# Two transformer layers on one core: a written order for the last groups, Sinkhorn scaling by two vectors, and a shifted sum in the mixing loop

## What is computed

```python
x = x + _L0_attn_ref(_layernorm(x), ...)   # 32 heads of 32, 8 key/value heads, causal, interleaved rope
x = x + _L0_ffn_ref(_layernorm(x), ...)    # the mixing layer
x = x + _L1_attn_ref(_layernorm(x), ...)   # the same attention, rope by halves
x = x + _L1_ffn_ref(_layernorm(x), ...)    # base matmul and 8 gated low-rank experts
```

```python
def sinkhorn_log(logits, num_iters=50, tau=0.1):
    Z = logits / tau
    def step(carry, _):
        u, v = carry
        u = -logsumexp(Z + v[..., None, :], axis=-1)
        v = -logsumexp(Z + u[..., :, None], axis=-2)
        return ((u, v), None)
    return exp(Z + u[..., :, None] + v[..., None, :])

H_res = (1.0 - g) * I + g * sinkhorn_log(H_res_logits)
y = einsum('btnc,btn->btc', x_streams, H_pre) @ W_branch
x_mixed = einsum('btij,btjc->btic', H_res, x_streams)
out = x_mixed + einsum('btc,btn->btnc', y, H_post)
```

## Time and profile before

| | |
|---|---|
| median of 3 runs | 2916.91 us |
| profiled execution, its own time | 2913.83 us |
| its span | 2912.1 us, 50930 instructions |
| PE busy | 2608.1 us (90%) |
| DVE busy | 1797.7 us (62%) |
| ACT busy | 1095.2 us (38%) |
| POOL busy | 1123.9 us (39%) |
| mean granted TensorE clock | 0.952 |
| attention 0, first score to last group's end | 116.4 to 958 us |
| mixing layer's Sinkhorn loop | 1203.9 to 1383 us |
| mixing loop | 1384 to 1464 us |
| attention 1, first score | 1582.8 us |

### The profile page before, as it was taken

One profiled execution on the slowest core, in us unless ns is written; L12 is line 12 of the kernel. 1 busy time (PEld: TensorE's weight loads), 2 busy tenths in 40 slices (PEclk: granted clock), 3 DMA queues, 4 the chain that ended last, 5 costly groups with the idle time before them and its releaser, 6 DMA issues. The chain is left out here.

```text
span 2912.1 us, 50930 instructions
## 1 busy us (share of the span) xinstructions
PE 2608.1 (90%) x15312; PEld 1828.1 (63%) x15312; DVE 1797.7 (62%) x4437; ACT 1095.2 (38%) x2381; POOL 1123.9 (39%) x801
## 2 busy tenths in 40 slices
PE   7999997999998799791969999979999987997999
PEld 6665653765654588681857565537656544876887
DVE  5677775667775433588756777765677753215543
ACT  2345454145555211470622454541354553002000
POOL 7456553546564100000054656545466642002110
PEclk9999998999999999896979999989999998998999
DMA  4323222422321421000244232213232314434111
GB/s 158 110 78 93 84 61 66 140 84 80 98 77 38 168 72 58 1 1 0 98 151 124 74 103 67 82 66 120 80 104 77 93 40 152 147 109 149 71 60 44
DMA packets 121086, 253.05 MB, mean 87 GB/s; under 512 B 12720, under 2 KB 39728, under 8 KB 120880
## 3 DMA queue, kind: packets, MB, share of 16 engines
q1 hardware_dynamic: 120912, 251.03, 27.0%
HBM read 166.57 MB, written 84.41 MB: 86 GB/s over the span
## 5 line engine op out<-in xcount | busy, mean ns | idle before, releaser
L617 ACT ACTIVATE a_prob<-a_pst 128x512 f32<-128x512 f32 (+3 forms) x1536 | 660.6, 493 | 560.4 <-PE a_pst L898 555.1
L710 DVE CUSTOM_DVE_ANT_0 a_psh<-a_psh,a_edge 128x128 f32<-128x128 f32 (+3 forms) x1024 | 479.7, 516 | 193.6 <-PE a_psh L851 172.6
L898 PE MATMUL a_pst<-a_qst,a_kst 128*128 128x512 f32 (+2 forms) x1536 | 487.9, 372 | 24.0 <-DMA a_qst<-rowmax 19.0
L851 PE MATMUL a_psh<-a_kst,a_qst 127*128 127x512 f32 (+3 forms) x1536 | 484.2, 363 | 16.2 <-DVE a_mx L710 6.1
L517 POOL TENSOR_TENSOR a_prob<-a_prob 128x2048 f32<-128x2048 f32 (+1 forms) x96 | 405.6, 4226 | 239.7 <-PE a_ppv L914 239.7
L851 PEld LDWEIGHTS a_psh<-a_kst,a_qst 127*128 127x128 f32 x1536 | 272.0, 189 | 229.8 <-DVE a_mx L713 92.7
L713 DVE TENSOR_REDUCE a_mx<-a_psh 128x1 f32<-128x512 f32 x512 | 329.1, 685 | 124.7 <-PE a_psh L851 123.7
L898 PEld LDWEIGHTS a_pst<-a_qst,a_kst 128*128 128x128 f32 x1536 | 287.5, 194 | 167.1 <-ACT a_prob L617 104.3
L914 PE MATMUL a_ppv<-a_prob,a_vg 128*32 128x512 f32 (+3 forms) x3072 | 319.8, 503 | 0.0
L502 POOL TENSOR_SCALAR_AFFINE_SELECT a_prob<-a_prob 128x512 f32<-128x512 f32 x256 | 161.8, 639 | 192.3 <-ACT a_prob L617 192.2
L927 PE MATMUL a_pden<-a_prob,a_ones 128*32 128x512 f32 (+3 forms) x2304 | 222.5, 479 | 14.1 <-POOL a_prob L517 14.1
(11 more groups left out here) (231 smaller groups left out, 4208.3 us busy)
## 6 DMA issues: line engine op xcount, KB each, us to landing
a_qst<-q SPq DMA_DIRECT2D x192, 256.0 KB, 4.5
a_wraw<-in_wqkv SPq DMA_DIRECT2D x52, 512.0 KB, 4.3
q<-a_stg_hi SPq DMA_DIRECT2D x64, 256.0 KB, 2.1
q<-a_stg_lo SPq DMA_DIRECT2D x64, 256.0 KB, 2.4
a_kst<-kT SPq DMA_DIRECT2D x96, 128.0 KB, 2.5
oT<-a_oT SPq DMA_DIRECT2D x32, 256.0 KB, 2.4
oT<-a_vT SPq DMA_DIRECT2D x32, 256.0 KB, 2.9
h_oraw<-oT SPq DMA_DIRECT2D x16, 512.0 KB, 4.0
```

The lines of the kernel that those rows point to most:

```text
L617: act.activation(prob[k % len(prob)][:, h, off:], pst[:, (k * GH + h) % 3, off:], ACT.Exp, scale=scale).then_inc(s["exp_done"], 1)
L710: part = dve.tensor_tensor_reduce(scores, scores, edge[:, BANK - n:], 1.0, 2 * MASKED, ALU.add, ALU.max, mx_hq[kc][:, h, qt:qt + 1])
L851: mm = pe.matmul(psh[:, at, i * n:(i + 1) * n], qst[par][0:P - 1, h, qt * P:(qt + 1) * P], kst[par][0:P - 1, kc * BANK:kc * BANK + n], sta ...
L898: pe.matmul(pst[:, (k * GH + h) % 3, off:], kst[par][:, ki * P:(ki + 1) * P], qst[par][:, h, qc * BANK + off:(qc + 1) * BANK], start=True, ...
```

## The change

Three edits.

1. ORDER_7, a text of its own, sets the last group of both batches; last_group() reads it, for body7 without its X and P steps. ("P:n.i" is P:next.i.) Rules and the branch of iteration() that made the old one are gone.
2. Sinkhorn keeps m unchanged in the loop and carries two vectors of 64 per partition, r64 for the rows and v64 for the columns. Each half multiplies m (or its transposed copy mt) by the other vector into e, sums e over rows and takes the reciprocal. After the loop m is multiplied by v64 and by r64, with the gate's factor in r64.
3. In the mixing loop DVE scales tile t + 1 before it adds PE's part to tile t. The first scaling and the last two sums stand outside the loop.

```diff
+ORDER_7 = """
+    ...
+    ST:3.0 XS:2 ST:3.1 ST:3.2 ST:3.3 XT:0 XL:3 D:0 XN:1 XC:0 XN:2 V:2
+    ...
+"""
...
-def iteration(full_s=True, proj=True, ahead=False):
+def iteration(proj=True):
...
+def last_group(ahead=False):
+    order = parsed(ORDER_7)
...
+    return order if ahead else [step for step in order if step[0][0] not in "XP"]
...
-    pro, bodies, body6, body7 = prologue(), (iteration(), iteration()), iteration(proj=False), iteration(False, False)
-    ahead7 = iteration(False, False, True)
+    pro, bodies, body6, body7 = prologue(), (iteration(), iteration()), iteration(proj=False), last_group()
+    ahead7 = last_group(ahead=True)
...
-            def normalise(axis):
-                dve.drain()
-                dve.tensor_reduce(r64[:, :, :], lines(m, axis), AX.X, ALU.add)
-                dve.drain()
-                dve.reciprocal(r64[:, :, :], r64[:, :, :])
-                dve.drain()
-                dve.tensor_tensor(lines(m, axis), lines(m, axis), spread(r64[:, :, :]), ALU.mult)
-            normalise("col")
+            def scale(kernel, other, out):
+                dve.drain()
+                dve.tensor_tensor(lines(e, "row"), lines(kernel, "row"), repeated(other[:, :, :]), ALU.mult)
+                dve.drain()
+                dve.tensor_reduce(out[:, :, :], lines(e, "row"), AX.X, ALU.add)
+                dve.drain()
+                dve.reciprocal(out[:, :, :], out[:, :, :])
+            dve.tensor_copy(lines(mt, "row"), lines(m, "col"))
+            dve.tensor_reduce(v64[:, :, :], lines(m, "col"), AX.X, ALU.add)
+            dve.drain()
+            dve.reciprocal(v64[:, :, :], v64[:, :, :])
             with dve.Fori(0, SINKHORN_ITERS - 1):
-                normalise("row")
-                normalise("col")
+                scale(m, v64, r64)
+                scale(mt, r64, v64)
             dve.drain()
-            dve.tensor_scalar(m[:, :, :], m[:, :, :], g[:, 2:3], None, ALU.mult)
+            dve.tensor_scalar(r64[:, :, :], r64[:, :, :], g[:, 2:3], None, ALU.mult)
+            dve.tensor_tensor(lines(m, "row"), lines(m, "row"), repeated(v64[:, :, :]), ALU.mult)
+            dve.drain()
+            dve.tensor_tensor(lines(m, "row"), lines(m, "row"), spread(r64[:, :, :]), ALU.mult)
             dve.drain()
...
             dve.wait_ge(s["xc"], NT)
-            with dve.Fori(0, NT // 2) as j:
+            scaled(0)
+            with dve.Fori(0, NT // 2 - 1) as j:
                 for par in range(2):
...
+                    scaled(j * 2 + par + 1)
+                    add_products(j * 2 + par, par)
+            scaled(NT - 1)
+            add_products(NT - 2, 0)
+            add_products(NT - 1, 1)
```

More of the change, by code:

```diff
@@ L92 @@
 """
+ORDER_7 = """
+    ST:0.0 ST:0.1 ST:0.2 XL:0 ST:0.3 XL:1
+    ST:1.0 ST:1.1 ST:1.2 ST:1.3 V:0 XL:2
+    ST:2.0 ST:2.1 ST:2.2 XS:0 XS:1 XN:0 V:1 ST:2.3
+    ST:3.0 XS:2 ST:3.1 ST:3.2 ST:3.3 XT:0 XL:3 D:0 XN:1 XC:0 XN:2 V:2
+    ST:4.0 D:1 ST:4.1 ST:4.2 XS:3 XT:1 XC:1 D:2 XL:4 V:3 ST:4.3
+    ST:5.0 ST:5.1 XS:4 XL:5 D:3 XT:2 XN:3 XC:2 ST:5.2 V:4 XN:4 ST:5.3 SUM:4+5
+    ST:6.0 ST:6.1 ST:6.2 XS:5 XT:3 XL:6 XC:3 ST:6.3
+    ST:7.0 V:5 ST:7.1 XS:6 XL:7 XN:5 XT:4 XC:4 ST:7.2 ST:7.3 D:4+5 V:6 XN:6
+    ST:8.0 SUM:6+7 ST:8.1 XT:5 XS:7 XC:5 ST:8.2 V:7 XN:7 ST:8.3
+    ST:9.0 ST:9.1 ST:9.2 XT:6 XC:6 ST:9.3 D:6+7 V:8
+    ST:10.0 ST:10.1 NORM:0 ST:10.2 SUM:8+9 ST:10.3
+    ST:11.0 ST:11.1 XT:7 XC:7 ST:11.2 ST:11.3 V:9 D:8+9 V:10 D:10 V:11 D:11 P:n.0 NORM:1 P:n.1 P:n.2
+      P:n.3 P:n.4 P:n.5 P:n.6 P:n.7
+"""
 def parsed(text):
     steps, k = [], 0
+    number = lambda x: "next" if x == "n" else int(x)
     for word in text.split():
@@ L104, in parsed @@
         elif what in ("ST", "P"):
-            steps.append((what, *(int(x) for x in rest.split("."))))
+            steps.append((what, *(number(x) for x in rest.split("."))))
         elif what in ("D", "SUM"):
@@ L109, in parsed @@
             steps.append((what, int(rest or 0)))
-    assert k == len(USES)
+    assert k in (0, len(USES))
     return steps
@@ L118 @@
 SUMS = [step[1] for step in STEPS if step[0] == "SUM"]
[L121 removed]
+def iteration(proj=True):
     left_out = set() if proj else {"P", "WL", "WS", "RK", "VG"}
[L127 to L156 removed]
+    return [step for step in STEPS if step[0] not in left_out and (proj or step not in (("HI", 0), ("LO", 0), ("RS", 0)))]
+def last_group(ahead=False):
+    order = parsed(ORDER_7)
+    assert [step[1] for step in order if step[0] == "D"] == DENS
+    assert [step[1] for step in order if step[0] == "SUM"] == SUMS
+    return order if ahead else [step for step in order if step[0][0] not in "XP"]
 def prologue():
@@ L1172, in mixing_layer @@
         r64 = sb("r64", [P, NT, NS])
+        v64 = sb("v64", [P, NT, NS])
+        mt = sb("mt", [P, NT, NS * NS])
         sums = sb("sums", [P, NT, 2])
@@ L1194, in spread, with repeated @@
             return v.unsqueeze(3).broadcast_to([P, NT, v.shape[2], n])
+        def repeated(v):
+            return v.unsqueeze(2).broadcast_to([P, NT, NS, NS])
         def tile(buf, t):
```

50 lines of the change are left out of this document (12 added, 38 removed).

## The result

| | before | changed |
|---|---|---|
| median on the same chip | 2915.97 us (4 runs, 2914.6 to 2921.62) | 2877.93 us (4 runs, 2876.34 to 2880.97) |
| profiled execution | 2913.83 us, span 2912.1 | 2876.36 us, span 2874.6 |
| mean granted clock | 0.952 | 0.961 |

A forecast was written before the change was run, and what follows sets the result against it. Bounds: TensorE waiting at low clock in layer 0's first-batch last group, DVE alone in Sinkhorn, DVE pacing the mixing loop. Terms -16.8 - 3.2 - 21.2 - 4.0 = -45.2 from 2913.8 gave 2869 us, range 2850 to 2890.

The forecast's parts named there:

- Sinkhorn, -16.8: Sinkhorn loop: row-order operands make every half 1.62 us, saving 17.6 us, less 0.8 behind the loop.
- The rival in which only the groups gain: Sinkhorn's multiplies keep the column price of 0.61 us, taking 17.6 us back: 2886 us, chance 0.04.
- First batches' last groups, -21.2: Last groups with the next batch's x rows: -12 in layer 0, -7.5 in layer 1, -1.7 for the clock.
- the walk: Layer 0's first-batch last group followed tile by tile: TensorE reaches the next projection's second chunk at 506 us.
- the mean: Second chunk in layer 0: 507.7 us, between 506 and 509.5 if XN:4 is caught too; 1.3 added for hops.
- The rival with five caught sums: Most normalises in first-batch last groups start behind a POOL sum, up to 4.2 us each: 2888 us, chance 0.2.
- Second batches' last groups, -4.0: Last groups of the second batches: the new order saves 1.5 us in layer 0 and 2.5 in layer 1.
- the one on SUM:8+9: Second batches' last groups: SUM:8+9 starts about 1.5 us earlier, ahead of D:8+9, which had waited 1.53.
- Mixing loop, -3.2: Mixing loop: scaling the next tile inside DVE's 4.52 us wait takes 3.7 us off the path once; bounds -1.5 and -4.5.
- every later tile does the same work: Mixing loop after the first tile: work unchanged, only some 0.1 us of address instructions more for each of 7 turns.
- The slower rival: Short TensorE gaps keep the first-batch last groups at the low clock, +25 in each layer: 2943 us, chance 0.03.
- The best case (2851): First-batch last groups lose no ties and TensorE is fed at full clock from tile 1 on: 2851 us, chance 0.12.

The follow-up runs named there:

- e1: The kernel before with the two-vector Sinkhorn alone; 2899.67 us, ratio 0.9935.
- e7: The changed kernel without the transposed copy mt, the second half multiplying m read by columns; 2879.16 us, ratio 0.9865.
- e2_order: The kernel before with ORDER_7 and last_group() alone; 2890.86 us, ratio 0.9909.
- e3: The kernel before with the shifted mixing loop alone; 2918.52 us, ratio 1.0005.
- e9: The kernel before with 32 idle DVE drains put at the start of the mixing layer; 2919.69 us, ratio 1.0018.
- e4: The changed kernel with XN:6 moved in front of XC:4; 2867.79 us, ratio 0.9830.
- e8: The changed kernel with the old order for the last groups of the second batches only; 2875.13 us, ratio 0.9861.

## Why the prediction was right, and where not

**Sinkhorn, -16.8: right.** Halves of 1.62 us as worked out; the piece gave 18.1 in the trace and 17.8 alone (e1). The price of the repeated operand, taken from a row of 384 elements, held (0.43). The step of 16 bytes is the gain: it cost 0.18 us in the reduce and 0.18 in the multiply of each of 49 turns, and e7, which pays the second again, loses 8.7. The rival in which only the groups gain, with multiplies at 0.61, is out.

**First batches' last groups, -21.2: right in mechanism, too small.** The second chunk was to come at 509 and came at 508.15, with the group 1.35 us later from its start. From a group's first score to that chunk it was 78.4 and is 64.3: -14.1 for the -12. Measured from the group's start the walk was close at each tile (tile 1's transposes at 18.8 us for 18.6, tile 6's at 40.2 for 40.8). XN:6 was caught as said (4.93 us, and 3.54 of waiting for tile 6, forecast 3.3); NORM:0, for which the walk had 2.6 us, ran free (0.69), and D:4+5 still waited, 0.40. The step that failed is the mean: the walk with XN:4 free gave 506, which is 63.5 from the group's start, and XN:4 did get ahead, by 0.22 us; averaging it with the caught case and adding 1.3 for hops took 3 us off. The caught case was not dearer either: e2_order's layer 1, where XN:4 was caught and XN:6 was not, has 63.9. In layer 1 73.6 became 64.5 (1942.16 less 1877.64): -9.1 for the -7.5. That smaller forecast rested on the distance of 73.6 us, and e1, e3 and e9, with the same order, have 77.9 to 78.0: one execution was taken for the kernel. Behind the chunk -1.2 and -2.3 were won, where half of 1.7 had been taken for each, for the clock. Together -26.7. (The bound on the good side stands as -39 in one place of the prediction and -36 in another; its 2850 goes with -36.) The rival with five caught sums fell, but the ties were real, and e4 shows the price of the one that was lost: 5.3 us in layer 0, 2.3 in layer 1.

**Second batches' last groups, -4.0: wrong.** They gave +1.9 and -1.5. The step that failed is the one on SUM:8+9: it looked at the last of the three sums alone (D:8+9 does wait less, 0.79 for 1.53, half of the 1.5 us forecast). The new order brings the other two D steps too near their sums. Before, in layer 0:

```profile
941.21 1.04 PE L927 MATMUL a_pden<-a_prob,a_ones 128*32 128x512 f32 x8
...
946.33 1.06 PE L927 MATMUL a_pden<-a_prob,a_ones 128*32 128x512 f32 x8 [0.25 <-POOL a_prob L517]
```

With the change:

```profile
929.07 1.06 PE L927 MATMUL a_pden<-a_prob,a_ones 128*32 128x512 f32 x8 [1.39 <-POOL a_prob L517]
...
935.92 1.06 PE L927 MATMUL a_pden<-a_prob,a_ones 128*32 128x512 f32 x8 [1.09 <-POOL a_prob L517]
...
941.73 1.07 PE L927 MATMUL a_pden<-a_prob,a_ones 128*32 128x512 f32 x8 [0.79 <-POOL a_prob L517]
```

Before, these waited 0, 0.25 and 1.53, now 1.39, 1.09 and 0.79: 1.49 us more. That would be most of layer 0's 1.9. In layer 1 the D steps wait just as long (1.39, 1.09 and 0.79), and the new order's 0.9 to 1.5 us there (37.0 in e8, 37.6 before, 36.1 changed) are not clear of the scatter.

**Mixing loop, -3.2: the wait went, the gain did not.** First wait and last wait are 1.72 + 0.71 for 4.52, so 2.1 us of waiting left the path (1.1 in e3). What was won stands at the end: behind the fifteenth tile's first sum 2.7 us are left where 5.6 were, and the first sum came 0.2 earlier. The step that failed is "every later tile does the same work", with 0.1 us a turn on top: the seven pairs between took 67.9 us for 66.1, most of them 9.78 in place of 9.43, which takes 1.9 back, and -1.2 is left. The first sum was to wait under 1 us and waited 1.72. Two thirds of the 0.35 us go with the place of the code (9.54 with 64 idle instructions, and then the stage takes 76.7 us for 79.6, -2.9); the 0.1 a turn that is left is of the size of the address work that had been allowed for, though the old loop moves as much by its place (9.57 in e9). And written out, both orders take the same 65.2 us between the sums: TensorE is then the bound, a case that the prediction did not look at, since it took DVE's arithmetic as given.

**What no step had: the second batch of attention 1, +10.1, and its first, -4.9.** The prediction gave layers that the change does not touch nothing at all. e3 and e9 show that edits ahead of them on DVE's instruction stream are enough. Without these 5.2 us net the changed kernel would stand near 2873. The 64-instruction shift, which costs 6.3 in the Sinkhorn piece and gives 10.0 in that batch and 1.7 in the mixing loop, ends at 2868.35.

**The slower rival** needed a last group at the low clock; it ran at 0.88. The best case (2851) needed no tie lost; one was. That the total came within 9 us of the forecast is in part luck: the first batches gave 5.4 us more than forecast, and a layer that the prediction left out took 5.2 back.

The sum in measured terms: -18.1 (Sinkhorn), -1.2 (mixing), -26.7 (first batches), +0.4 (second batches), +5.2 (attention 1's ordinary groups), +2.2 (attention 0's, 1.2 and 1.0, of the size that they scatter by between runs), +0.7 elsewhere: -37.5.

What stays open: why DVE's second stop is longer at one place than at another, and why layer 1's last first-batch group was quicker in the trace of before than in three others. A kernel that aligns each DVE loop by itself was not tried, so what is lost to the place of the code altogether is not known.

## What to carry to other kernels

When an edit is timed, compare untouched stages too: here 5 to 10 us moved in a layer that the edit doesn't reach, because it shifted a loop's code, and idle instructions put ahead show it. One trace is one execution: a row that a forecast rests on is worth a look in a second trace (148.3 us here, 151.5 to 151.7 in three others). Where two engines start within 0.2 us of each other on a port that one can hold, order them so that the short one goes first: a 0.8 us step moved one place forward was worth 10 us, 7.6 of them where it stands. And a wait removed from an engine that isn't quite the bound buys nothing when the real cost is the address arithmetic of its loop; writing the loop out was worth 5 us there, and 15 in all with what it moved elsewhere.
